# A graph network on one core: bf16 one-hots with the tile innermost, the sort's edge network staged half a group apart, and a last layer with another order of work

## The reference

```python
# layer 1: attention over edges, an edge network of three layers on 64 attributes
h = silu(edge_attr_64 @ W_fc1 + b_fc1); h = silu(h @ W_fc2 + b_fc2); w = h @ W_fc3 + b_fc3
tp = (msg_src[src] + msg_dst[dst]) * edge_weight * w
k, v = split(tp @ W_kv + b_kv); alpha = (q[dst] * k).sum(-1)        # softmax by dst
out1 = segment_sum(v * softmax(alpha), dst) @ W_proj + b_proj
# layer 2: out = segment_sum(h[src] * dinv[src] * dinv[dst], dst), over edges in both directions and loops
# layer 3: copy_sum = segment_sum(f[src], dst); inner_sum = segment_sum(f[src] * f[dst], dst)
# layer 4: logits = leaky_relu(s[src] + d[dst] + edge_attr_16 @ a_edge), both directions and loops
#          out = segment_sum(softmax_by_dst(logits) * xt[src], dst)
x = layernorm(x + out)                                               # after each
```

## Time and profile before

| | |
|---|---|
| median of 3 runs | 20287.62 us (20268.27 to 20302.71) |
| the profiled execution's own time | 20324.25 us |
| its span | 20322.5 us |
| busy: PE, PEld | 11661.4 us (57%), 8792.1 us (43%) |
| busy: DVE | 11590.8 us (57%) |
| busy: ACT, POOL | 4433.7 us (22%), 8939.4 us (44%) |
| granted clock of PE, mean | 0.625 of full speed |

### The profile page before, as it was taken

The page is one execution under the profiler, slowest core; times in us unless marked ns, Lnnn a source line. Parts: engine busy times, 40 slices in busy tenths (PEclk is TensorE's granted clock), DMA queues, the critical chain, the costliest instruction groups (busy, mean ns, idle before and its releaser), DMA issues. The chain is left out here.

```text
span 20322.5 us, 328487 instructions
## 1 busy us (share of the span) xinstructions
PE 11661.4 (57%) x72558; PEld 8792.1 (43%) x72559; DVE 11590.8 (57%) x36905; ACT 4433.7 (22%) x11783; POOL 8939.4 (44%) x9490
## 2 busy tenths in 40 slices
PE   4555555555554666665575665655555664447776
PEld 3433333333333555554475443332224663226775
DVE  7955655665553333333564777782365556776666
ACT  0011111111110222221111341005301113435554
POOL 0055655655551555555672444430262444332222
PEclk8766666666665666666555655555555655557777
DMA  7421221222122222223233996547543776654444
GB/s 313 188 62 61 64 62 61 64 63 62 60 62 68 57 58 58 58 58 56 54 58 39 305 304 207 169 134 221 178 130 96 240 239 205 210 190 156 153 147 128
DMA packets 2091763, 2590.62 MB, mean 127 GB/s; under 512 B 839927, under 2 KB 1708736, under 8 KB 2091624
## 3 DMA queue, kind: packets, MB, share of 16 engines
q1 hardware_dynamic: 1737832, 1933.77, 31.5%
q0 software_dynamic: 353792, 655.45, 10.8%
HBM read 1738.72 MB, written 849.42 MB: 127 GB/s over the span
## 5 line engine op out<-in xcount | busy, mean ns | idle before, releaser
L549 POOL DMA_INDIRECT edges_by_dst<-rec,pos x1568 | 1557.2, 993 | 2581.1 <-DVE rec L484 2006.4
L976 POOL DMA_INDIRECT sc_rows<-src_table,sc_idx x1664 | 1585.1, 953 | 1431.9 <-DVE sc_tp L1074 770.9
L549 POOL DMA_INDIRECT edges_by_cell<-rec,pos x1568 | 1552.0, 990 | 526.3 <-issue 524.5
L1806 PE MATMUL gs_part<-gs_rows,gs_oh 128*128 128x192 bf16 x6528 | 1234.3, 358 | 907.0 <-DVE gs_oh L1779 621.5
L1720 PE MATMUL ex_rows<-table,ex_oh 128*128 x6528 | 1168.9, 348 | 909.3 <-DVE ex_oh L1688 414.1
L1768 POOL DMA_INDIRECT gs_rows<-rows_by_src,chunk_read_by_src x1088 | 1128.5, 1037 | 960.0 <-PE gs_part L1806 673.4
L2203 PE MATMUL at_part<-at_oh,key_in_block 128*66 128x128 f32 x8704 | 1328.1, 322 | 378.4 <-issue 195.3
L2203 PEld LDWEIGHTS at_part<-at_oh,key_in_block 128*66 128x66 f32 x8704 | 1229.7, 169 | 471.7 <-issue 423.7
L1026 PE MATMUL sc_loc<-dst_table,sc_ohT 128*128 x3328 | 760.5, 400 | 1091.4 <-ACT sc_ohT L992 1028.8
L1806 PEld LDWEIGHTS gs_part<-gs_rows,gs_oh 128*128 128x128 bf16 x6528 | 741.4, 131 | 1399.9 <-issue 824.2
L1720 PEld LDWEIGHTS ex_rows<-table,ex_oh 128*128 128x128 bf16 x6528 | 757.5, 132 | 1320.5 <-issue 1281.4
(11 more groups left out here) (391 smaller groups left out, 27369.5 us busy)
## 6 DMA issues: line engine op xcount, KB each, us to landing
ex_keys<-src_key_rows SPq DMA_DIRECT2D x1632, 128.0 KB
rows_by_src<-ex_stage SPq DMA_DIRECT2D x1088, 192.0 KB
rowb<-sort_key_rows SPq DMA_DIRECT2D x392, 512.0 KB
ex_keys<-dst_key_rows SPq DMA_DIRECT2D x1088, 128.0 KB
dst_rows_by_src<-patY SPq DMA_DIRECT2D x1, 104448.0 KB, 272.4
gs_rows<-dst_rows_by_src SPq DMA_DIRECT2D x544, 192.0 KB
scored_dst_rows_by_src<-patZ SPq DMA_DIRECT2D x1, 71808.0 KB, 448.0
scored_rows_by_src<-ex_stage SPq DMA_DIRECT2D x544, 132.0 KB
```

The lines of the kernel that those rows point to most:

```text
L549: nc.gpsimd.indirect_dma_start(out=out, out_offset=bass.IndirectOffsetOnAxis(ap=pos[:, u, k, j:j + 1], axis=0), in_=row, in_offset=None).t ...
L976: nc.gpsimd.indirect_dma_start(out=rows[:, u, j, :], out_offset=None, in_=tabS, in_offset=bass.IndirectOffsetOnAxis(ap=idx[:, u, j:j + 1], ...
L1806: m = nc.tensor.matmul(part[k][u][:, 0, :], oh[k][:, u % 2, r, :], rows[k][:, u, r, :], start=r == 0, stop=r == SLOTS - 1)
```

## The change

**One-hots.** `K.iotab` becomes `K.iota4` [128, 128, 4]: each number four times in a row. Every bf16 one-hot that compares two tensors is written with tiles (or slots) innermost: two in histogram and sort, four in `sum_rows`. The key's broadcast moves from the innermost to an outer dimension. PE and L526 of the sort then read a one-hot with a pitch of 4 bytes (histogram, sort) or 8 bytes (`sum_rows`). The order of hi and lo halves in `hilo` and `onehot` changes with it.

**Edge network.** Group g+1's attributes are transposed at c = 2 of group g, fc1 runs at c = 0, fc2 at c = 2, fc3 at c = 0 of the group after. The last group's fc3 runs after the loop, whose last body is written apart.

**Last layer.** Four arrays `tops` in place of `top`, each update waits for the one four before; key rows of `at3` are loaded three quads ahead into two buffers; `AHEAD` is 3; DVE's order of pieces is another, and its fp32 one-hots lie in `K.ecA`. Keys `keyA`, `keyB`, `KB` are bf16.

```diff
-    K.iotab = sb("iotab", [P, P], BF16)
+    K.iota4 = sb("iota4", [P, P, SLOTS], BF16)
...
+                            def keys(half):
+                                return hilo[:, bass.ds(g, 1), half, :, :].rearrange("p o k (q t) -> p (o k q) t", t=2)
                             nc.vector.tensor_tensor(
-                                onehot[:, u, :, 0, :, 0:NB], bcast(bcast(K.iotab[:, 0:NB], 1, [P, SG, NB]), 1, [P, 2, SG, NB]),
-                                bcast(hilo[:, bass.ds(g, 1), :, 0, :].rearrange("p o k t -> p (o k) t"), 3, [P, 2, SG, NB]), ALU.is_equal)
+                                onehot[:, u, HI, :, 0:NB, :], bcast(K.iota4[:, 0:NB, 0:2], 1, [P, 2 * PAIRS, NB, 2]),
+                                bcast(keys(HI), 2, [P, 2 * PAIRS, NB, 2]), ALU.is_equal)
...
                 nc.vector.tensor_tensor(
-                    onehot[:, u, k, h, half:half + SG // 2, :], bcast(K.iotab[:, :], 1, [P, SG // 2, P]),
-                    bcast(hilo[:, bass.ds(g, 1), k, h, half:half + SG // 2].rearrange("p o t -> p (o t)"), 2, [P, SG // 2, P]),
-                    ALU.is_equal).then_inc(s_one, 1)
+                    onehot[:, u, h, first:first + PAIRS // 2, :, :], bcast(K.iota4[:, :, 0:2], 1, [P, PAIRS // 2, P, 2]),
+                    bcast(hilo[:, bass.ds(g, 1), h, k, half * (SG // 2):(half + 1) * (SG // 2)].rearrange("p o (q t) -> p (o q) t", t=2), 2,
+                          [P, PAIRS // 2, P, 2]), ALU.is_equal).then_inc(s_one, 1)
...
+def tile_onehot(onehot, u, half, k, j):
+    return onehot[:, u, half, k * PAIRS + j // 2, :, j % 2]
...
-                        nc.vector.tensor_tensor(oh[k][:, u % 2, :, :], bcast(K.iotab[:, :], 1, [P, SLOTS, P]),
-                                                bcast(keys[:, bass.ds(g, 1), :].rearrange("p o r -> p (o r)"), 2, [P, SLOTS, P]),
+                        nc.vector.tensor_tensor(oh[k][:, u % 2, :, :], K.iota4[:, :, :],
+                                                bcast(keys[:, bass.ds(g, 1), :].rearrange("p o r -> p (o r)"), 1, [P, P, SLOTS]),
...
+                def attrs(g, u, loaded):
+                    pe.wait_ge(s_ea[u], loaded * 64)
+                    pe.wait_ge(s_rec, g + 2)
+                    for q in range(SG // 2):
+                        m = nc.tensor.transpose(xps[u][:, q * P:(q + 1) * P],
+                                                ea[:, u, 2 * q:2 * q + 2, :].rearrange("p t c -> p (t c)"), K.ident[:, :])
+                    m.then_inc(s_xt, 1)
...
                             if c == 0:
-                                pe.wait_ge(s_ea[u], (i + 1) * 64)
-                                pe.wait_ge(s_rec, g + 2)
...
+                                fc1(g, u)
+                                if not (isinstance(g, int) and g == 0):
+                                    fc3(g - 1, v)
                             if c == 1:
                                 pe.wait_ge(s_one, (g + 1) * NK + 2)
                                 turn(g + 1, v)
...
                             if c == 2:
...
+                                fc2(g, u)
+                                if not (last and u == 1):
+                                    attrs(g + 1, v, i + 1 + u)
+                loop(pe, NG // 2, body)
+                fc3(NG - 1, (NG - 1) % 2)
...
                         nc.scalar.activation(h2[:, :], xps[u][:, :], ACT.Silu, bias=bb[:, 1:2]).then_inc(s_h2, 1)
+                        if not (last and u == 1):
+                            attrs(g + 1, v)
...
-AHEAD = 2
+AHEAD = 3
...
-                            wait(dve, s_top, q * 2 * QUAD + e)
+                            wait(dve, s_top, q * 2 * QUAD + 2 * v + k - 3)
...
-                skewed(sp, n, [(1, load_rows), (2, load)])
+                skewed(sp, n, [(1, load_rows), (3, load)])
...
-                skewed(dve, n, [(2, turned), (1, arguments), (0, sums), (1, first_onehots)], blocks)
+                skewed(dve, n, [(0, sums(0, 2)), (1, arguments), (0, sums(2, 4)), (2, turned(0)), (0, sums(4, 6)), (2, turned(1)), (0, sums(6, E)),
+                                (1, first_onehots)], blocks)
```

More of the change, by code:

```diff
@@ L29 @@
 LOOKS = 2
+LO, HI = 0, 1
 CLAMPED = "clamped to the nodes' blocks where it is made"
@@ L569, in _, with body @@
                 nc.scalar.activation(warm[:, :], keycol[:, 0, 0, 0:1], ACT.Silu)
-                with act.Fori(0, NG // 2) as i:
+                attrs(0, 0)
+                def body(i, last):
                     for u in range(2):
@@ L602, in _, with body @@
                 added(0, [(0, 0), (0, 1)])
-                with pe.Fori(0, NG // 2) as i:
+                attrs(0, 0, 1)
+                def body(i, last):
                     for u in range(2):
@@ L1805, in products @@
                         for r in range(SLOTS):
-                            m = nc.tensor.matmul(part[k][u][:, 0, :], oh[k][:, u % 2, r, :], rows[k][:, u, r, :],
+                            m = nc.tensor.matmul(part[k][u][:, 0, :], oh[k][:, u % 2, :, r], rows[k][:, u, r, :],
                                                  start=r == 0, stop=r == SLOTS - 1)
@@ L2114, in sb @@
             return ctx.enter_context(nc.sbuf_tensor(f"{name}_{nm}", s, d))
-        keys = [sb(f"keys{k}", [P, QUAD, SLOTS * P], BF16) for k in range(2)]
+        keys = [sb(f"keys{k}", [P, 2, QUAD, SLOTS * P], BF16) for k in range(2)]
         ohT = [sb(f"ohT{k}", [P, 2, QUAD, SLOTS * P], BF16) for k in range(2)]
@@ L2246, in first_onehots, with sums, run @@
                         onehots(i * RING + u, e)
-                def sums(i, u):
-                    q = i * RING + u
-                    for e in range(E):
-                        if e + AHEAD < E:
-                            onehots(q, e + AHEAD)
-                        k, v = e // QUAD, e % QUAD
-                        wait(dve, s_mm, q * E + e + 1)
-                        wait(dve, s_acc, q * E + e)
-                        b = held[k][u * QUAD + v]
-                        nc.vector.tensor_tensor(accT[:, bass.ds(b, 1), :], accT[:, bass.ds(b, 1), :], part[e % RING][:, :, :], ALU.add).then_inc(s_acc.sem, 1)
+                def sums(first, end):
+                    def run(i, u):
+                        q = i * RING + u
+                        for e in range(first, end):
+                            if e + AHEAD < E:
+                                onehots(q, e + AHEAD)
+                            k, v = e // QUAD, e % QUAD
+                            wait(dve, s_mm, q * E + e + 1)
+                            wait(dve, s_acc, q * E + e)
+                            b = held[k][u * QUAD + v]
+                            nc.vector.tensor_tensor(accT[:, bass.ds(b, 1), :], accT[:, bass.ds(b, 1), :], part[e % RING][:, :, :], ALU.add).then_inc(s_acc.sem, 1)
+                    return run
                 def blocks(i):
@@ L2576, in build @@
         sd = sb("s_and_d", [P, 2, NB], F32)
-        top = sb("top", [P, NB], F32)
         M3 = sb("node_maxima", [P, NB, 3], BF16)
```

129 lines of the change are left out of this document (69 added, 60 removed).

## The result

The changed kernel takes 19281.03 us in the median (19258.8 to 19293.95, 4 runs) against 20287.07 before: a ratio of 0.9503, 95% interval 0.9487 to 0.952. That is 1006 us less. The profiled execution took 19293.05 us, its span 19291.3 us.

The account below looks back on a forecast made before the run. It took each changed stage to have its own bound: DVE in histogram, no single engine in sort or at3. Gains 230 + 290 + 90 + 140 + 400 + 100 = 1250 us gave 19040 us, range 18440 to 19750.

Parts of the forecast that it names:

- Rival D: All changed bf16 one-hots: they gain nothing, a key's outer stride of zero counting as before; about 19700 us, chance 0.08.
- Rival A: Histogram and sort: runs of two still read slowly, costing two thirds of the doubling; 19210 us, chance 0.13.
- stages that this change leaves alone: Peeled loop, bf16 keys, moved order of `hilo`: put at nothing, as outside the loops or in such stages.
- take 90: gs2: one one-hot a group would give 147 us, but POOL needs 750 of 853; 90 taken, bounds 0 and 110.
- The wait it named: mx3: DVE's 0.20 us between updates of `top`, 181 us in all, goes; 140 taken, bounds 60 and 181.
- The third list ahead: at3: products asked for one list sooner, against PE's 165 us of waiting for one-hots; part of the 400 us.
- scatter, load and 1.25 groups: Sort: 21.7 + 7.1 = 28.8 us must fit in 1.25 groups, holding a group at 23 us or more.
- above 210: Sort: sign that PE's wait at the attribute transposes would exceed 210 us; over 600 would mean B or E.
- rival B: Sort: the attribute chain lengthens it by 2 us a group, PE waiting at c = 2; 19540 us, chance 0.16.
- burst and lag alternate: Sort: DVE starts late during long scatter bursts with nothing to wait for, so neither DVE nor POOL alone is the bound.
- Rival C: Sort: comes near POOL's limit, 23.4 us a group, PE's waits having held DVE; 18440 us, chance 0.15.
- Rival E: Sort: PE held at c = 2 for 7.1 us in every group, so slower than before; 20530 us, chance 0.04.

Follow-up runs that it names:

- e4_fill_late: Changed kernel with fills of tables that only layers 2 to 4 use moved to ACT's DMA queue, waited for at the sort's end: 19156 us, ratio 0.9434.
- e2_sp_order: Changed kernel with SP loading the sort's attributes of group g+2 ahead of the wait for scatters, then waiting for those of g-1: 19280 us, ratio 0.9493.
- e8_no_cell: Changed kernel without the scatters of edges_by_cell (8 of 16 a group), SP's order unchanged: 17521 us, ratio 0.8587, sort's loop 3159 us.
- e1_staging_back: Changed kernel with the sort's edge network staged as before, all in one group: 19254 us, ratio 0.948.
- e3_back_sp_order: Changed kernel with the edge network staged as before and SP's attribute loads ahead of the wait for scatters: 19303 us, ratio 0.9502.
- e5_quarters: Changed kernel with SP's early attribute loads, and POOL pausing after every four scatters until they land: 19773 us, ratio 0.9688, sort's loop 5427 us.
- e9_pauses_all: Changed kernel with late fills, SP's early attribute loads, and POOL pausing after each group's eighth and last scatter: 19031 us, ratio 0.9353.
- e6_halves: Changed kernel with SP's early attribute loads, and POOL pausing after each group's eighth scatter: 19195 us, ratio 0.9408, sort's loop 4834 us.

## Why the prediction was right, and where its steps were off
Forecast 19040 in 18440 to 19750; measured 19281. Of the 1250 us forecast 1006 came.

- **Price of a one-hot:** 422 ns forecast, 421 and 422 measured. Rival D fell with it. Rival A fell too: 4 bytes of every 8 are read at 0.52 ns an element, and no penalty of the kind that the Trainium skill's Vector Engine (DVE) Microarchitecture Reference (5.2, The SBUF access granule: adjacent pairs) gives for hops of single words is seen here; the page's rows are for streams of 32-bit elements. L304 of the kernel before, now L307, was put near 1220 ns and took 1294 (its shortest 1218). One reason is not separated: in `sum_rows` the change made the keys bf16 as well (`keyA` and `keyB`, fp32 before), which the text put at nothing ("stages that this change leaves alone"), though gs1 and gs2 compare these very keys. So in gs1 the price may hang on the type, on the layout or on both. In histogram and sort `hilo` was bf16 before too, and there the layout alone did it.
- **Histogram:** the sort's first work at 730 us forecast, 734.7 measured. DVE itself was ready at 581 and not at 620, which gained nothing. That the fills come last next was shown by `e4_fill_late`, whose moved fills let it start at 593.
- **gs1:** 290 forecast, 268 measured. PE's wait for one-hots fell from 443 to 188 us.
- **gs2:** 90 forecast, 13 measured. The step "take 90" priced the stage's slack over POOL's own time as if DVE's saving could use it. POOL is busy 523 us of 840 after the change, so it was not full; its wait for PE grew instead (119 to 199 us) with DVE's wait for products. Which part of the gather's round trip holds it was not tried.
- **mx3:** 140 forecast, 78 measured. The wait it named went fully; the waits behind it (PE, 69 us; the last maximum, 22) took half of it back, which the text had named and sized too small.
- **at3:** 400 forecast, 300 measured: 12.1 us a quad, where 11.4 was taken. The order of DVE's pieces carries some 130 of it; the rest, some 170, is left for the key rows, which no run changed by themselves. The third list ahead, which the sum counted, carries none that could be seen.
- **Sort:** 100 forecast, 157 measured, and for a reason that the step did not have. It said that attributes wanted sooner would hold a group, and priced scatter, load and 1.25 groups at 23 us a group. The wait did come (1926 us; "above 210" was the text's sign of it), and the text's sign of rival B, over 600, was met too; yet it cost nothing, as SP's order showed in `e2_sp_order` and again in `e8_no_cell`. Nor did the waits for ACT that the staging covers bring anything (`e1_staging_back`, `e3_back_sp_order`). The row that decided was the one on DVE's lag in the earlier trace rows, which the prediction read ("burst and lag alternate") and then gave no term. The 157 us are what is left of the six one-hots' 6 x 0.27 x 196 = 315 us of DVE's work: `e1_staging_back`, whose sort differs from the kernel before in the one-hots and their layout alone, took 5075 us from first to last scatter where the kernel before took 5249. That the forecast of 100 lay near is luck: its gain was to come from staging too, and its price was for a chain that did not bind.
- **Rival C** would have needed the lag gone; without it the limit is POOL's bursts and pauses, as the runs with pauses show. **Rival E** fell: the wait of 1926/187 = 10 us a group was longer than its 7.1 and did not count.

## What to carry to other kernels
A wait that grows ninefold may cost nothing: before work is moved to cover it, take it away in a run and see if the engine that it feeds waits less. Where one engine issues long trains of indirect DMAs, count what the others start in each few us of a train, since a pause on the issuing engine can pay for itself. Here a comparison of two bf16 tensors ran at twice the rate (512 elements in 422 ns, 689 before) once no operand had an innermost step of zero, and what that brings is read stage by stage from who waits for DVE.

## What the runs showed of the hardware that was not expected
After about 10 us of scatters issued without a pause (0.96 us each, 0.30 between), DVE started 9 instructions in 11 us where it had started 54, with DMA engines at a share of 0.06. It recovered about 3 us after the burst. With bursts of four scatters and pauses of 2.7 us nothing of this was left. What is held up inside the chip no run tells; the trace shows no instructions being loaded meanwhile. DVE was also busy less for the same 15360 instructions where bursts were short: 2646 us in `e5_quarters` and 2711 in `e9_pauses_all`, against 2789 in the changed kernel and 2812 in `e6_halves`.
